# Second-layer operands begun 12 steps sooner in every second step, their roots by VectorE, and VectorE making the last five products with the scales in a two-layer transformer kernel

## What is computed

```
# layer 0: one-head attention, then an FP4 feed-forward
x = x + ga * (softmax(q k^T / sqrt(128)) v @ Wout + bout)
def fp4_quant_dequant(x):            # blocks of 16 values
    scale = maximum(max(abs(xb)) / 6.0, 1e-12)
    return _GRID[searchsorted(_MID, abs(xb / scale))] * sign(xb) * scale
h = silu(fp4(x) @ fp4(w_gate).T) * (fp4(x) @ fp4(w_up).T)
x = x + gb * (fp4(h) @ fp4(w_down).T)
# layer 1: attention of 16 heads with a bias from lines, then a feed-forward of 4 ternary matmuls
L = p1[_PI] * p2[_PJ] - p1[_PJ] * p2[_PI];  line = L / max(norm(L), 1e-12)
logits = q k^T * scale + (read_lines . J write_lines) * decay ** (i - j) * bias_scale    # causal
```

## Time and profile before

| | us |
|---|---|
| three runs | 1043.72, 1046.60, 1048.62 (median 1046.60) |
| the profiled execution | 1043.87, its span 1042.6 |
| busy in the span: PE, DVE, ACT, POOL | 867.4, 746.9, 657.5, 406.3 |
| layer 0 ends (gate) | at 324.84 |
| step 148 to the gate | 226.1 to 324.84 |
| mean granted TensorE clock | 0.946 of full speed |

### The profile page before, as it was taken

One profiled execution on the slowest core, in us unless ns is written; L12 is line 12 of the kernel. 1 busy time (PEld: TensorE's weight loads), 2 busy tenths in 40 slices (PEclk: granted clock), 3 DMA queues, 4 the chain that ended last, 5 costly groups with the idle time before them and its releaser, 6 DMA issues.

```text
span 1042.6 us, 25479 instructions
## 1 busy us (share of the span) xinstructions
PE 867.4 (83%) x9999; PEld 529.3 (51%) x9999; DVE 746.9 (72%) x1784; ACT 657.5 (63%) x1154; POOL 406.3 (39%) x664
## 2 busy tenths in 40 slices
PE   5688888876465798998989899898978868898987
PEld 2344455554343465665656566565555533444434
DVE  4776888898585778677786877868878547666554
ACT  4668888746133365756566575665656747685866
POOL 3043455456865544373553645444232210101000
PEclk8899999998766699999999999999999989999999
DMA  5000000000324262543425334261552000000000
GB/s 148 22 1 1 1 1 1 1 1 3 103 65 117 67 169 50 127 122 88 130 66 138 81 98 120 66 171 47 133 145 65 3 1 1 21 2 21 1 22 21
DMA packets 70698, 63.60 MB, mean 61 GB/s; under 512 B 30600, under 2 KB 62824, under 8 KB 70576
## 3 DMA queue, kind: packets, MB, share of 16 engines
q1 hardware_dynamic: 70064, 61.90, 22.1%
q10 hardware_dynamic: 512, 0.02, 0.0%
HBM read 34.02 MB, written 27.36 MB: 59 GB/s over the span
## 4 chain that ended last, share of the span: by engine, by line
PE 45%; DVE 11%; issue 6%; ACT 5%; POOL 2%; DVEq 0%; POOLq 0%; ACTq 0%
PE bank L2081 12%; PE bank L1662 7%; PE bank L1637 3%; PE bank L1610 3%; PE bank L1602 3%; PE bank L1618 3%; PE bank L1599 2%; PE bank L1592 2%; DVE bank L1745 1%; ACT 4g L2139 1%; PE bank L1628 1%; DVE 4f L2175 1%; PE bank L1670 1%; PE bank L1625 1%; DVE roots L1299 1%
## 5 line engine op out<-in xcount | busy, mean ns | idle before, releaser
L1823 ACT ACTIVATE ET<-bank 64x512 f32<-64x512 f32 x128 | 75.5, 590 | 102.3 <-PE bank L1628 101.5
L2162 DVE TENSOR_TENSOR act<-4f,act 128x512 f16<-128x512 f32 x96 | 66.4, 691 | 57.7 <-ACT act L2129 57.5
L1818 ACT ACTIVATE ET<-bank 128x768 f32<-128x768 f32 x128 | 103.2, 806 | 2.3
L1745 DVE TENSOR_TENSOR bank<-bank,W 128x256 f32<-128x256 f32 x128 | 54.7, 427 | 51.6 <-PE bank L1592 51.6
L1750 DVE TENSOR_TENSOR bank<-bank,WT 128x256 f32<-128x256 f32 x128 | 55.3, 432 | 49.9 <-PE bank L1618 49.9
L1755 DVE TENSOR_REDUCE mo<-bank 128x4 f32<-128x512 f32 x128 | 87.8, 686 | 2.7 <-PE bank L1602 2.5
L1662 PE MATMUL bank<-ET,vv 128*32 128x128 f32 (+2 forms) x1792 | 89.1, 323 | 0.8 <-DVE O L1780 0.8
L2129 ACT ACTIVATE act<-4f 128x512 f16<-128x512 f32 x96 | 60.4, 630 | 28.6 <-DVE 4f L2175 26.6
L1763 DVE TENSOR_REDUCE mo<-bank 128x3 f32<-128x384 f32 x128 | 70.0, 547 | 0.0
L1764 DVE TENSOR_REDUCE mo<-bank 128x3 f32<-128x384 f32 x128 | 70.0, 547 | 0.0
L1602 PE MATMUL bank<-maskq,identh 128*64 128x512 bf16 x256 | 62.7, 396 | 0.0
(11 more groups left out here) (377 smaller groups left out, 2539.7 us busy)
## 6 DMA issues: line engine op xcount, KB each, us to landing
ring<-scr_q SPq DMA_DIRECT2D x16, 324.0 KB
QO<-scr_q SPq DMA_DIRECT2D x16, 324.0 KB
ring<-scr_a SPq DMA_DIRECT2D x16, 252.0 KB
KA<-scr_a SPq DMA_DIRECT2D x16, 252.0 KB
ring<-scr_k SPq DMA_DIRECT2D x16, 168.0 KB
KB<-scr_k SPq DMA_DIRECT2D x16, 168.0 KB
scr_a<-dk SPq DMA_DIRECT2D x8, 288.0 KB, 2.6
X<-in_x SPq DMA_DIRECT2D x8, 256.0 KB, 4.9
```

Source lines behind the costliest of these rows:

```text
L1745: dve.tensor_tensor(half(psD, 1), half(psD, 1), over(W[:, h * HB:(h + 1) * HB], NT), ALU.mult).then_inc(s_wq, 1)
L1818: act.activation(ET[n % NE][:, T:SEG * P], psXT[:, 0:NP * P], ACT.Exp).then_inc(s_expo, 1)
L1823: act.activation(to[0:HB, :], psDT[0:HB, :], ACT.Exp)
L2162: dve.tensor_tensor(lo, f32_[f % 3], hi, ALU.subtract).then_inc(s_lo, 1)
```

## The change

1. The slots begin at step 147 and take every second step: 147 + 2k for piece k (TensorE, and now GpSimd too), one later for VectorE and ScalarE. Before it was about 159 + 1.5k. Piece 0 is 12 steps sooner, piece 10 now 7 or 8, piece 13 now 5, piece 16 now 4, piece 19 now 2 or 3, piece 26 none.
2. What needs the attention's memory waits for its last residual only from slot 12 on (GpSimd, ScalarE); TensorE waits for its last projection of v; wo of layer 0 moves from 3xh to the tile dqn. The zeroing stays at steps 160 to 167.
3. Batch 0's Newton rounds and the product behind them run on VectorE (slots 14 and 15). Those of batches 1 to 7 stay on GpSimd.
4. For x >= 11 VectorE makes the product of half x with the scales in its own tenth step, at step 69 + 9x: 168, 177, 186, 195, 204.

```diff
-    FREE = 159
+    BEGIN, FREE = 147, 159
+    LINES = 12
...
-        q, r = divmod(f - FREE - behind, 3)
-        n = 2 * q + r - ahead.slots
-        return n if r < 2 and -ahead.slots <= n < 0 else None
+        q, r = divmod(f - BEGIN - behind, 2)
+        return q - ahead.slots if r == 0 and 0 <= q < ahead.slots else None
...
         if n == -ahead.slots:
-            pe.wait_ge(first.s_add, B)
+            pe.wait_ge(first.s_v, B)
...
     def slot_act(f):
         n = operands_slot(f, 1)
-        if n == -ahead.slots:
+        if n == LINES - ahead.slots:
             act.wait_ge(first.s_add, B)
...
     def slot_pool(f):
-        n = operands_slot(f, 1)
-        if n == -ahead.slots:
+        n = operands_slot(f, 0)
+        if n == LINES - ahead.slots:
             pool.wait_ge(first.s_add, B)
...
     def half_dve(x):
         yield from quantise_dve(dve, half(x), 2 * FF // 16, tmps_b[x % 2], s_hstep, x, [(s_prod, 2 * x + 2)], (s_hq, x - 1) if x >= 2 else ())
+        if x >= BY_DVE:
+            quantise_pool(dve, hq[x % 2], 2 * FF // 16, tmps_b[x % 2], s_hstep, x, s_hq, (s_turn, 2 * (x - 1)))
...
     def half_pool(x):
         yield from blank(9)
-        quantise_pool(pool, hq[x % 2], ...)
+        if x < BY_DVE:
+            quantise_pool(pool, hq[x % 2], ...)
...
-        yield from blank(3)
+        yield
+        if b == 0:
+            dve.wait_ge(s_rn, 1)
+            yield from newton(dve, b)
+        else:
+            yield
+        yield
...
+    def newton(eng, b):
+        for i in range(3):
+            for k, (x_, y_) in enumerate(((rn, rn), (nh, n2))):
+                eng.tensor_tensor(nh, x_, y_, ALU.mult).then_inc(s_newton, 1)
+                eng.wait_ge(s_newton, 12 * b + 4 * i + k + 1)
+            eng.tensor_scalar(nh, nh, -0.5, 1.5, ALU.mult, ALU.add).then_inc(s_newton, 1)
+            eng.wait_ge(s_newton, 12 * b + 4 * i + 3)
+            eng.tensor_tensor(rn, rn, nh, ALU.mult).then_inc(s_newton, 1)
+            eng.wait_ge(s_newton, 12 * b + 4 * i + 4)
+            if i == 1:
+                yield
+        Lv = L.rearrange("p (s i h) -> p s i h", s=8, i=NL)
+        eng.tensor_tensor(Lv, Lv, rn..., ALU.mult).then_inc(s_Ln, 1)
```

More of the change, by code:

```diff
@@ L616, in attention0 @@
     first.s_x, first.s_rest, first.s_chans, first.s_rows = s_x, s_rest, s_chans, s_rows
-    first.pe, first.dve, first.act, first.pool, first.s_add, first.signals = on_pe, on_dve, on_act, on_pool, s_add, signals
+    first.pe, first.dve, first.act, first.pool, first.signals = on_pe, on_dve, on_act, on_pool, signals
+    first.s_v, first.s_proj, first.s_add = s_v, s_proj, s_add
     return first
@@ L835, in ffn0 @@
     ENDS = MAIN + CYCLE * B + 12
+    BY_DVE = 11
     def together(weights, rows, hidden, half):
@@ L917, in half_pool @@
         yield from blank(9)
-        quantise_pool(pool, hq[x % 2], 2 * FF // 16, tmps_b[x % 2], s_hstep, x, s_hq, (s_turn, 2 * (x - 1)) if x >= 2 else ())
+        if x < BY_DVE:
+            quantise_pool(pool, hq[x % 2], 2 * FF // 16, tmps_b[x % 2], s_hstep, x, s_hq, (s_turn, 2 * (x - 1)) if x >= 2 else ())
         if x % 2:
@@ L977, in slot_dve @@
         n = operands_slot(f, 1)
+        if n in (-ahead.slots, H - ahead.slots):
+            dve.wait_ge(second.s_add, (n + ahead.slots) // H + 1)
         if n is not None:
[L979 to L982, removed]
             ahead.dve(n)
@@ L1105, in attention1 @@
     units = dk_[0:3, 0:G * KX // 2]
-    first_weights = roots, xh[:, 0:D], c.sb("bq", 2, at=held), s_w0
+    first_weights = roots, dqn_.bitcast(F32)[:, 0:D], c.sb("bq", 2, at=held), s_w0
     first_room = raw_.bitcast(F32)[:, 0:T], raw_.bitcast(F32)[:, T:2 * T], L[:, 0:T], sq[:, 0:T]
@@ L1372, in operands_act @@
             yield
+    def newton(eng, b):
[10 more added lines that the diff above has]
+        Lv = L.rearrange("p (s i h) -> p s i h", s=8, i=NL)
+        eng.tensor_tensor(Lv, Lv, rn.rearrange("p (s o h) -> p s o h", s=8, o=1).to_broadcast([P, 8, NL, H]), ALU.mult).then_inc(s_Ln, 1)
     def operands_pool(b):
@@ L1422, in operands_pool @@
         yield from blank(2)
[L1423 to L1434, removed]
+        if b:
+            pool.wait_ge(s_rn, b + 1)
+            yield from newton(pool, b)
+        else:
+            yield
         yield from blank(4)
```

## The result

The changed kernel took 1037.6 us (median of 7 executions) beside 1043.7 for the kernel before (7): the ratio of times on record is 0.992, with an interval of 0.990 to 0.994 (the two medians alone give 0.994). A second set on another occasion gave 0.995 (0.993 to 0.997). Over all sets together the medians are 1038.6 (13 executions) and 1045.7 (80 executions): about 7 us, 0.7%, against a forecast of 5.5; by the first set alone it is 6 us by the medians and 8 by the ratio. The profiled execution took 1037.2, its span 1036.0, 6.6 less than before.

A forecast was written before the change was run, and what follows sets the result against it. The bound was the chain to layer 0's end gate, mainly VectorE and GpSimd waiting in turn. Its terms put the gate at 319.3 instead of 324.84, 5.5 us sooner: 1038.4 profiled, 1041.1 median, range 1035.5 to 1046.5.

The forecast's parts named there:

- steps 148 to 158, VectorE later: At 226.1 to 240.2 us VectorE takes over batch 0's statistics, with no gap to hide them: 1.4 us later.
- M begins: In steps 159 to 174 ScalarE's last cp limits GpSimd's M, which starts at 255.2; before, the cp ended at 264.06.
- Holes, common queue, roots: Up to L1312: VectorE's holes fill, it shares one queue with GpSimd, roots take 4.1 us; L1312 6.7 us sooner.
- The price of a turn over the engines (1.9): From the end of batch 0's roots to L1312, the same turn as before: 1.9 us.
- the stop for raw: VectorE's wait ahead of L1312, 6.96 us before, was to be near 1.5.
- GpSimd nearly without idle time from 240 to 265: A sign expected in the profile: GpSimd hardly idles between 240 and 265 us.
- L1312 to Y of half 13: This stretch takes 17.3 us instead of 14.5, bounds 16 to 19; Y at 299.8, 3.9 us sooner.
- The tail: From L654 of half 15 to the gate: VectorE's product saves 0.92 us, the rest stands, leaving 8.15.
- the first rival: Filled holes keep TensorE's clock at 2.4 GHz, 1.5 us in the tail; gate 8 to 8.5 sooner, 1038.4; chance 0.2.
- Behind the gate: Layer 1, from the gate to the end: no change from 717.8 us, with bounds of -1.5 to +1.5.
- The second rival: Small GpSimd instructions hold up VectorE for their full length, so the kernel is slower, 1050.3; chance 0.1.
- the third (M late, 2.3 us): M starts late, the sums of squares start at 272.5, the gate comes 2.3 us sooner, 1044.3; chance 0.2.

The follow-up runs named there:

- y_raw: The changed kernel with batch 0's second L1334 one slot sooner, in step 184 instead of 186; median 1039.7 us, ratio 0.993 to the kernel before.
- e_roots: The kernel before with only batch 0's roots moved to VectorE, slots and products as before; ratio 0.999 (0.997 to 1.000).
- e_products: The kernel before with only the last five products moved to VectorE, old slots and roots on GpSimd; ratio 0.999 (0.998 to 1.001).
- c_heads: The changed kernel with six more 128 x 128 TensorE products in each of the first 12 turns of layer 1's loop; ratio 0.995 to the kernel before.
- e_slots: The kernel before with only the new slots and their waits, roots and all products on GpSimd; ratio 0.995 (0.994 to 0.997).

## Why the prediction was right and where not

| term | forecast | measured |
|---|---|---|
| steps 148 to 158, VectorE later | 1.4 | 1.3 (L651 to L534 11.33 against 10.05) |
| M begins | 255.2 | 256.5 |
| L1299 | 269.3 | 269.8 |
| end of the roots | 280.5 | 281.4 |
| L1312 | 282.5 | 283.3 |
| Y of half 13 | 299.8 | 301.95 |
| L654 of half 15 ends | 311.1 | 312.9 |
| tail to the gate | 8.15 | 6.70 |
| gate | 319.3 | 319.6 |
| gate sooner | 5.5 | 5.2, or 5.8 counted from L518 |
| behind the gate | 717.8 | 716.4 |

*Holes, common queue, roots.* Right to about a microsecond. The price of a turn over the engines (1.9) came as 1.87, the roots took 0.29 where two tensors are multiplied and 0.23 where not, in sum 3.7 + 0.96 for the forecast 3.1 + 0.95, and the stop for raw stayed at 1.3 for the forecast 1.5. The reading that VectorE and GpSimd form one queue carried it: the old stop ahead of L1299 went down to 1.75 (the sign asked for under 1.5), and M, L and sq took 13.3 us beside VectorE's work (256.48 to 269.77), and 11.5 before with half 12's product between them. The sign "GpSimd nearly without idle time from 240 to 265" did not come: it stood 3.93 us for cp and was busy for 17.59 of 23.60. L664 on VectorE took 0.88 to 1.84 us, median 1.16; half 14's cost 1.84 and not 0.83, beside a GpSimd addition that ran until 306.32.

*L1312 to Y of half 13: the first step that failed.* "TensorE's turn, projections and product of this place do not move with it" and a wait of 1.5: the wait was 3.27 and the part 18.6 us instead of 17.3. I looked at ScalarE's rows as what TensorE starts from, as in before, and did not count that L1334 frees TensorE's bank; as the second instruction behind the new product of half 13 (1.24, held up) it ended at 295.42, 1.8 us after ScalarE's rows. y_raw shows that start. It cost 1.3 here and with the smaller lags ahead of it made L654 2.8 sooner instead of 4.7.

The sentence also missed an order. In before TensorE turned half 13's product ahead of batch 1's rows:

```profile
294.19 0.84 PE L875 MATMUL bank<-ident,hq 128*128 128x128 f32 x3
298.67 1.12 PE L1243 MATMUL bank<-ident,3xh 128*128 128x128 f32 x4 [3.64 <-ACT 3xh L1330]
```

The new slots put the rows' turn at step 187 instead of 189, ahead of half 13's first turn at 188. So the rows' turn did move, from 298.67 to 295.57, but half 13's product, ready at 294.03, now stands behind it and is turned at 296.19, and from the rows' turn to Y it takes 6.38 us instead of 5.04. No run takes this order back, so what it costs is not shown.

*The tail: the second step that failed, the other way.* "The rest of the tail stands", so 8.15: it took 6.70. The product was right (0.89 for 0.92 where nothing holds it up). What did not stand was TensorE's part, at a granted clock of 1.00 where before had 0.62: a net 1.48 of the tail's 2.37, the first rival's mechanism and its 1.5. That rival was held to be 0.2 likely. The clock of the tail was 0.56 to 0.62 in all five profiles with the old slots and no extra TensorE work (three of before, e_roots, e_products). It was 0.95 to 1.00 in seven of the eight with the new slots, half 15's product on VectorE and no extra work ahead of the gate; c_heads, 0.63, is the eighth. So the change brings the full clock here in most executions, and not in all. Why is not shown.

*Behind the gate*: no change was taken, and 1.4 us came, inside the bound of 1.5, in a part that the change does not touch. It is the third term by which the time is off.

So the near hit of the gate, 5.2 for 5.5, is in part luck: two errors of opposite sign, 1.8 us late up to L654 and 1.45 gained in the tail. The time fell by about 7 and not by 5.5, since the clock in the tail (1.5) and the part behind the gate (1.4) were left out of the sum and the loss ahead of Y of half 13 took back only part. The forecast's size is too small by over a fifth, and those 3 of the 7 us are of a kind that differs between executions. The second rival (VectorE held up, slower) fell with e_slots; the third (M late, 2.3 us) as well, L1299 being at 269.8; SyncE, whose last issue ended at 317.4, was 2.3 us ahead of the gate.

## What to carry to other kernels

When work moves off a waiting engine, look first at whether the other engine still idles once the remaining edits are in: the roots were worth 3.2 us of the gate alone and nothing that the profiles show beside the new slots. A hole filled on one engine ends at the next thing that another engine waits for, so list for every moved instruction what it frees (here a PSUM bank) as well as what it makes. List too which of two instructions of one engine comes first now. Compare parts by distances between two marks in one profile when executions differ by more than the part is worth; set the first mark ahead of everything that the change moves, and see first how much the distance differs for identical code (1.5 us here).

## What the runs showed of the hardware

- VectorE and GpSimd hold each other up at some instructions: the same product on VectorE took 0.88 to 1.84 us, GpSimd's M piece of 128 x 192 took 0.59 at 256.48 and 1.24 at 257.03 in the changed kernel. That they take turns, instruction by instruction, is my reading of these rows.
- The granted TensorE clock differs between two executions of the same instructions: 1.00 and 0.63 in a tail of 7 to 8 us, worth 1.5 us net.
- Extra TensorE work to hold the clock up did raise it (0.62 to 1.00 in the tail of before). It gained 0.9 us at the gate there, and in the changed kernel the gate came 2.4 and 5.3 us later. I take the reason to be that TensorE's products are in a chain with the other engines.
